# Four layers of cross attention on one core: value products of layer 0 in four column groups, operands laid out transposed ahead of the launch, and first waits moved to their first use

## What is computed

```python
h = jnp.concatenate([x, latents], axis=1)                  # x: the layer's 256 tokens, latents: see below
q = (latents @ q_w + q_b).reshape(b, k_len, NH, DH)        # 16 heads of 16
kv = (h @ kv_w + kv_b).reshape(b, p + k_len, NH, DH, 2)
kmat, v = (kv[..., 0], kv[..., 1])
attn = jnp.einsum('bkhd,bnhd->bhkn', q, kmat) / DH
attn = jnp.where(full_mask[:, None, None, :], attn, -jnp.inf)
attn = jax.nn.softmax(attn.astype(jnp.float32), axis=-1)
attn_out = jnp.einsum('bhkn,bnhd->bkhd', attn, v).reshape(b, k_len, H)
attn_out = attn_out @ out_w + out_b + residual
out = rmsnorm(attn_out, postnorm_w)
out = jax.nn.gelu(out @ mlp_w1 + mlp_b1) @ mlp_w2 + mlp_b2
return out + residual
```

## Time and profile before

| | us |
|---|---|
| median of 3 runs | 861.67 (860.86 to 862.11) |
| the profiled execution's own time | 862.19 |
| span of its profile | 860.5 |
| PE busy | 766.9 (89%) |
| DVE busy | 535.8 (62%) |
| ACT busy | 407.8 (47%) |
| POOL busy | 364.4 (42%) |

### The profile page before, as it was taken

The page is one execution under the profiler, slowest core; times in us unless marked ns, Lnnn a source line. Parts: engine busy times, 40 slices in busy tenths (PEclk is TensorE's granted clock), DMA queues, the critical chain, the costliest instruction groups (busy, mean ns, idle before and its releaser), DMA issues.

```text
span 860.5 us, 12877 instructions
## 1 busy us (share of the span) xinstructions
PE 766.9 (89%) x4759; PEld 593.1 (69%) x4759; DVE 535.8 (62%) x1035; ACT 407.8 (47%) x965; POOL 364.4 (42%) x384
## 2 busy tenths in 40 slices
PE   3899999999849978868999998999998799776798
PEld 2788887887729835546775677877577689444598
DVE  3565666657484459976553768333789647299644
ACT  1677685876522237764563322664223131266421
POOL 2565453545450148876221765000666603267300
PEclk8999999999969999999999999999999989997899
DMA  7400000000000050000254000232000000200000
GB/s 192 133 2 2 1 1 1 2 2 1 2 0 1 16 180 1 1 1 1 99 194 150 1 0 1 74 123 99 1 0 1 1 0 2 97 1 1 1 17 34
DMA packets 26050, 30.86 MB, mean 36 GB/s; under 512 B 3628, under 2 KB 20868, under 8 KB 25988
## 3 DMA queue, kind: packets, MB, share of 16 engines
q1 hardware_dynamic: 25448, 30.03, 10.8%
q10 hardware_dynamic: 540, 0.01, 0.0%
HBM read 28.98 MB, written 1.05 MB: 35 GB/s over the span
## 4 chain that ended last, share of the span: by engine, by line
PE 67%; DVE 15%; issue 7%; POOL 6%; ACT 3%; DMA 2%; ACTq 1%; SPq 0%; POOLq 0%; DVEq 0%
PE wide_ps L440 9%; PE narrow_ps L459 8%; PE narrow_ps L611 7%; PE wide_ps L758 7%; PE wide_ps L487 6%; PE narrow_ps L793 5%; PE wide_ps L709 5%; PE wide_ps L745 3%; PE wide_ps L732 3%; POOL probs L1521 2%; DVE scoresb L1231 2%; DVE mx L1240 2%; DVE sums L1247 2%; PE wide_ps L420 2%; PE wide_ps L589 2%
## 5 line engine op out<-in xcount | busy, mean ns | idle before, releaser
L916 ACT ACTIVATE probsT<-wide_ps 128x640 f32<-128x640 f32 (+1 forms) x104 | 86.0, 827 | 135.6 <-PE wide_ps L487 134.7
L1513 POOL TENSOR_TENSOR scoresb<-scoresb,mx 128x768 f32<-128x768 f32 (+1 forms) x40 | 70.7, 1767 | 151.9 <-DVE mx L1238 113.5
L1535 POOL TENSOR_TENSOR probs<-scoresb,rcp 128x512 f32<-128x512 f32 (+1 forms) x128 | 91.3, 735 | 77.9 <-DVE rcp L1315 77.9
L487 PE MATMUL wide_ps<-ident,probs 128*128 128x128 f32 x640 | 90.7, 280 | 30.0 <-POOL probs L1521 24.3
L487 PEld LDWEIGHTS wide_ps<-ident,probs 128*128 128x128 f32 x640 | 73.4, 144 | 56.7 <-issue 54.7
L1499 POOL TENSOR_TENSOR rstd<-veps,mhalf 128x1 f32<-128x1 f32 x56 | 32.0, 572 | 139.2 <-DVE veps L1166 139.2
L611 PE MATMUL narrow_ps<-probsT,vpad 128*64 128x128 f32 x640 | 83.4, 278 | 1.4 <-ACT xq L916 1.4
L1521 POOL TENSOR_TENSOR probs<-scoresb,rcp 128x1024 f32<-128x1024 f32 x40 | 78.1, 1954 | 7.3 <-DVE rcp L1248 7.3
L611 PEld LDWEIGHTS narrow_ps<-probsT,vpad 128*64 128x64 f32 x640 | 68.2, 136 | 13.7 <-issue 11.0
L440 PE MATMUL wide_ps<-xq_r,wstream_r 128*128 128x512 f32 x192 | 66.0, 427 | 8.8 <-issue 7.0
L459 PEld LDWEIGHTS narrow_ps<-wstream_r,hidden 128*128 128x128 f32 x576 | 69.2, 188 | 1.2 <-DVE xB L1194 0.5
(11 more groups left out here) (167 smaller groups left out, 1567.4 us busy)
## 6 DMA issues: line engine op xcount, KB each, us to landing
wstream<-in_L_xattn_wk SPq DMA_DIRECT2D x8, 512.0 KB, 4.1
wstream<-in_L_xattn_wv SPq DMA_DIRECT2D x8, 512.0 KB, 5.2
wstream<-in_L_xattn_wo SPq DMA_DIRECT2D x8, 512.0 KB, 6.1
wstream<-in_wqT SPq DMA_DIRECT2D x8, 512.0 KB, 7.0
wstream<-in_L_xattn_mlp_w SPq DMA_DIRECT2D x2, 1024.0 KB, 6.3
wstream<-in_L_xattn_w_fc SPq DMA_DIRECT2D x2, 1024.0 KB, 6.2
xq<-in_x SPq DMA_DIRECT2D x1, 1024.0 KB, 6.1
wstream<-in_L_xattn_fc_w SPq DMA_DIRECT2D x1, 1024.0 KB, 4.9
```

The lines of the kernel that those rows point to most:

```text
L487: m = nc.tensor.transpose(ps[:, j * P:(j + 1) * P], probs[:, u % 2, j * P:(j + 1) * P], ident[:])
L916: nc.scalar.activation(dst, src, ACT.Identity, **kw).then_inc(ring.drained[ring.slot(key)], 1)
L1513: g.tensor_tensor(s3[:, first:], s3[:, first:], mx[:, u % 3, first:].unsqueeze(2).broadcast_to([P, 16 - first, n_scores]), ALU.subtract).t ...
L1535: g.tensor_tensor(probs[:, u % 2, o:o + 2 * n].rearrange("p (i k) -> p i k", i=2), s3[:, :, lo:hi], rcp[:, u % 3, 0:2].unsqueeze(2).broadc ...
```

## The change

1. `x`, the context, the doubled context and a 128 x 384 table of all parameter columns are laid out in transposed form by `kernel()` before the launch, together with `kv_w` split into keys and values, and the ten bias rows in one array. They are loaded straight into `actT`, `ctxT`, `ctxD`, `col`, `rows`. The transposes by PE, their copies by ACT, the doubling by POOL and the zeroing of `colraw` are gone; so are the 35 loads of single vectors and nine of the ten row loads. `cols`, `ctxT` and `mask0i` are issued by ACT, the rest by SP.
2. Waits for loads stand at the first use of each tensor. 16 transposes of the identity by itself stand at the head of PE's program, one small activation at the head of ACT's.
3. The units run in the order b, half of the heads c, query half q, head pair j of four. `values0` is called every fourth step, for four units: 20 matmuls of 32 columns, the four head pairs in turn on output partitions 0, 32, 64, 96, accumulated over 5 matmuls each. The transposed probabilities stay in six buffers (`turned_probs`). `vpad0` holds 32 columns a head instead of 64.
4. Context values are made for two batches at a time (`vctx`), all at the start. The keys are spread in six pieces (`PIECES`) instead of five, the sixth in the first step of its own batch.
5. POOL adds the bias rows inside the loop (steps 4 to 19); the zeroing of `vpad0` waits for DVE's zeroing of `qhot`; `mask3` is made behind the first MLP.

```diff
-        units0 = [(b, r, q) for b in range(B) for r in range(H0 // 2) for q in range(2)]
+        units0 = [(b, 4 * c + j, q) for b in range(B) for c in range(NC) for q in range(2) for j in range(4)]
...
-        SIDE0 = [("q",), ("proj", 0), ("proj", 1), ("k", 0), ("k", 1), ("qhot", 0), ("qhot", 1), ("kpair", 0),
-                 ("kpair", 1), ("qhot", 2), ("kpair", 2), ("kpair", 3), ("qhot", 3), ("kpair", 4), ("v", 0), ("v", 1)]
...
+        SIDE0 = [("kpair", 5), ("proj", 0), ("proj", 1), ("q",), ("k", 0), ("k", 1), ("qhot", 0), ("kpair", 0),
+                 ("kpair", 1), ("qhot", 1), ("kpair", 2), ("v",), ("qhot", 2), ("kpair", 3), ("qhot", 3), ("kpair", 4)]
+        PIECES = [(0, 512), (512, 1024), (1024, 1280), (1280, 1792), (1792, 2304), (2304, 2560)]
+
+        START0 = [[("q",), ("k", 0), ("qhot", 0), ("kpair", 0), ("kpair", 1), ("qhot", 1), ("kpair", 2)],
+                  [("v",), ("vctx", 0), ("vctx", 1), ("k", 1), ("qhot", 2), ("kpair", 3), ("kpair", 4), ("qhot", 3),
+                   ("kpair", 5)]]
...
             pe.wait_ge(consts, 1)
-            pe.wait_ge(load["x"], 16)
-            turn("x0T", xA)
...
-            pe.wait_ge(load["w0"], 16 * 3)
-            pe.wait_ge(*wide.empty("ctxT"))
+            for i in range(16):
+                nc.tensor.transpose(wide_ps[:, 2, 0:P], ident[:], ident[:])
+            pe.wait_ge(load["q_w0"], 16)
...
+                elif kind == "vctx":
+
+                    ps, filled = take_narrow((job, b), 4, among)
+                    pe.wait_ge(load["ctxD"], 16)
+                    for i in range(2):
+                        for kc in range(NC):
+                            m = mm(ps[:, i * D:(i + 1) * D], ctxD[:, kc, 2 * job[1] + i, :, :].rearrange("p a k -> p (a k)"),
+                                   kv_w0[:, kc, 1, :], start=kc == 0, stop=kc == NC - 1)
...
+                for k in range(5):
+                    i, kb = k // 2, k % 2
+                    for j in range(4):
+                        r = 4 * c + j
+                        h = 2 * r + i
+                        lhs = (vpad0[b % 2][:, kb * 512 + h * 32:kb * 512 + (h + 1) * 32] if k < 4 else
+                               vctx0[b][:, r * 32:(r + 1) * 32])
+                        m = mm(ps[32 * j:32 * j + 32, qoff(q)], lhs, turned_probs(4 * group + j)[:, k * P:(k + 1) * P],
+                               start=k == 0, stop=k == 4)
...
-                if 0 <= step - 1 < n0:
-                    values0(step - 1)
+                if step > 0 and step % 4 == 0:
+                    values0(step // 4 - 1)
...
+            sp.dma_start(*halves(q_w0, t["L0_xattn_q_w"])).then_inc(load["q_w0"], 16)
+            sp.dma_start(actT[:, :, 0:S], xT[:, :, 0:S]).then_inc(load["xT0"], 16)
...
+            act.dma_start(col[:].rearrange("p a n -> p (a n)"), t["cols"]).then_inc(load["cols"], 16)
+            act.dma_start(ctxT[:], t["ctxT"].rearrange("(c p) n -> p c n", p=P)).then_inc(load["ctxT"], 16)
...
+            pool.wait_ge(qhot_zeroed, 1)
+            for lo, hi in ((0, 2048), (2048, 3072)):
+                g.memset(vpad_mem[:, lo:hi], 0.0).then_inc(vzero, 1)
...
+                if 4 <= step < 4 + NQ:
+                    add_row(step - 4, xB, xA, "L0_out_b")
+                if step == 4 + NQ:
+                    pool.wait_ge(row_added, NQ)
+                if 4 + NQ <= step < 4 + 2 * NQ:
+                    add_row(step - 4 - NQ, xA, xA, "L0_mlp_b2")
```

More of the change, by code:

```diff
@@ L60, with column_table @@
         "L3_cproj_b", "L3_proj_b"]
+def column_table():
+    at, n = {}, 0
+    for name, k in COLUMNS:
+        if n // P != (n + k - 1) // P:
+            n = -(-n // P) * P
+        at[name] = (n, k)
+        n += k
+    return at
 class Ring:
@@ L585, in scores0 @@
                     pe.wait_ge(*narrow.empty((("qhot", r // 2), b)))
-                    for piece in range(r * KEYS0 // 512, -(-(r + 1) * KEYS0 // 512)):
-                        pe.wait_ge(*narrow.empty((("kpair", piece), b)))
+                    for piece, (lo, hi) in enumerate(PIECES):
+                        if lo < (r + 1) * KEYS0 and hi > r * KEYS0:
+                            pe.wait_ge(*narrow.empty((("kpair", piece), b)))
                 for i in range(2):
@@ L633, in _ @@
                     side_product0(job, b, SIDE)
-            pe.wait_ge(load["cols"], 16 * LOADS["cols"])
-            ps, filled = take_wide("cols")
-            for i in range(2):
-                m = nc.tensor.transpose(ps[:, i * P:(i + 1) * P], colraw[:, 1 + i, :], ident[:])
-            m.then_inc(filled, 1)
+            pe.wait_ge(load["cols"], 16)
             pe.wait_ge(wk_ready, 2)
@@ L859, in _ @@
             sp.dma_start(mask3i, t["mask_BxS2_bf1"].rearrange("(a b) k -> a (b k)", a=1).broadcast_to([P, B * T])).then_inc(load["masks"], 16)
             sp.dma_start(mask1[:], t["mask_Bx1xSxS2_ff0"].rearrange("b o (h p) k -> p (b o h) k", p=P)).then_inc(load["masks"], 16)
-            for i, name in enumerate(ROWS):
-                key = name[:3] + "xattn_" + name[3:]
-                sp.dma_start(rows[:, i, :], t[key].rearrange("(a d) -> a d", a=1).broadcast_to([P, D])).then_inc(load["rows"], 16)
@@ L864, in _ @@
-            sp.wait_ge(cols_zeroed, 1)
-            for dst, src, apart in parameter_rows(False):
-                sp.dma_start(dst, src, allow_slow_non_contiguous=apart).then_inc(load["cols"], 16)
             sp.dma_start(*halves(mlp_load(0, 0), t["L0_xattn_mlp_w1"])).then_inc(load["mlp0"], 16)
@@ L959, in probs_turned @@
                 n = 5 if u < len(units0) else 8
-                evac(probsT[:, u % 2, 0:n * P], wide_ps[:, wide.slot(key), 0:n * P], wide, key)
+                evac(turned_probs(u)[:, 0:n * P], wide_ps[:, wide.slot(key), 0:n * P], wide, key)
             def side0_copy(job, b):
                 key = (job, b)
-                if job[0] in ("proj", "v"):
+                if job[0] in ("proj", "v", "vctx"):
                     return
@@ L968, in side0_copy @@
                 if job == ("qhot", 0) and b == 0:
-                    act.wait_ge(placed, 6)
+                    act.wait_ge(qhot_zeroed, 1)
                 ps = narrow_ps[:, narrow.slot(key), :]
                 if job[0] == "kpair":
-                    evac(kpair[:].rearrange("p r k -> p (r k)")[:, 512 * job[1]:512 * (job[1] + 1)], ps, narrow, key)
+                    lo, hi = PIECES[job[1]]
+                    evac(kpair[:].rearrange("p r k -> p (r k)")[:, lo:hi], ps[:, 0:hi - lo], narrow, key)
                 elif job[0] == "qhot":
@@ L1015, in keys_small @@
                     evac(kT2[:, c, :], wide_ps[:, wide.slot(key), c * 256:(c + 1) * 256], wide, key, bias=column(kb, c))
[L1017 to L1022 removed]
+            act.wait_ge(consts, 2)
+            nc.scalar.activation(rcp[:, 0, 0:1], mhalf[:], ACT.Identity)
+            act.wait_ge(load["cols"], 16)
             for job in START0[0]:
@@ L1286, in side0_copy @@
                 if job[0] == "qhot":
+                    if job == ("qhot", 0) and b == 0:
+                        dve.wait_ge(qhot_zeroed, 1)
                     v.tensor_copy(qhot[0:64, 2 * job[1]:2 * job[1] + 2, 0, :],
```

219 lines of the change are left out of this document (87 added, 132 removed).

## The result

The changed kernel takes **840.45 us** (839.04 to 842.74, 4 runs) against 861.26 (860.5 to 862.11, 4 runs): ratio 0.974, 95% interval 0.9718 to 0.9763. It is faster, as forecast, but by 21 us in place of 36, and the median is just beyond the end of the range (840). The profiled execution took 840.74 us (span 839.0) against 862.19 before: 21.45 less.

What follows compares the result with a forecast made beforehand. Waits bound the start, PE batches 0 to 2, a loop through ACT, DVE and POOL batch 3. Savings of 11.1 + 6.5 + 17.0 + 1.2 + 0.3 = 36.1 us from 862.2 gave 826.1 us, range 815 to 840.

Steps and rivals of the forecast that it cites:

- The value group: Layer 0's value products in column groups: 40 records at 0.036 us, 1.44 us in every fourth step instead of 4.96.
- the start: Stretch before the first transposes of batch 0: earlier loads and fewer waits, 11.1 us less, ends 7 to 13.5.
- POOL's row additions: Bias additions of 0.73 us each between POOL's normalizations in batch 0: priced at nothing, up to 3 us if uneven.
- batch 3 would keep its loop: Layer 0's batch 3 stays paced by the two-unit loop through ACT, DVE and POOL: 1.2 us less, 0 to 2.5.
- OVERLAP: Follow-up theory on value products: neighbours in different column groups make them cheap; without that, 3 to 4.5 us per group.
- my own case: Whole kernel: the summed savings come about as priced, 823 to 835 us; chance 55%.
- rival B: Whole kernel: in-order queues cost more, batches of 47 us, row additions 3, start 7; 19 less, 843 us; chance 15%.
- Batches 1 and 2, +4.9: Layer 0's batches 1 and 2: 43.0 us each against 51.5, together 17.0 us less, ends 21 to 9.
- all side jobs share one narrow tile: Layer 0's batches: the second key product waits while DVE empties the shared tile, 0.7 us a batch.
- the two projections: Layer 0's projection steps: POOL waits at the norm's root before the next normalization, twice; steps 1 to 4 become 2.4 us longer.
- Unchanged at about 634 us: Sign for the stretch from layer 0's last unit to the end: same length, the 7 us normalization still in it.
- 7 us faster if DVE came first: Behind layer 0, POOL's two long products hold DVE's last normalization 7.13 us; the other order would be 7 us faster.

Runs made afterwards that it cites:

- the experiment: Changed kernel with each group's 20 value products written unit by unit instead of going round the four column groups: 878.27 us.
- three remedies: Changed kernel with identity turns in batch 3, POOL's reciprocal root one step later, and layer 1's keys spread in MLP gaps: 818.04 us, ratio 0.9476.
- all places: Kernel of three remedies, first key pieces earlier, layer 3's keys in later pieces, identity turns before MLPs and layer 2's key products: 808.9 us, ratio 0.9379.

## Why the prediction was right, and where it failed

**Right.** The value group (1.44 taken, 1.23 measured, and shown by the experiment to hang on the column groups), the start (-11.1 taken, -12.4 measured; 6.3 for the first query product, 5.87 measured), and POOL's row additions at nothing. That batch 3 would keep its loop and give nearly nothing was right in kind: at full clock and with the root moved it takes 36.8 against 37.2. The sign was never close, since OVERLAP holds in chains of five.

**Half right.** 840.45 does not lie in my own case (823 to 835, 55%) but where I had put rival B (835 and above, 15%). B's own prices did not come: no batch took 47 us (44.8 and 46.1), the row additions cost nothing and the start gave 12.4 in place of 7. What came is a part of its mechanism, the waits in order, and a loss that no rival had.

**Slips that changed nothing.** Batch 3's two terms, 11 times 0.05 and 12.7 less 11.9, add to 1.35 and not to 1.2. VectorE's zeroing, put at 7.7, ended at 8.3.

**The step that failed** most stood in no term: I let TensorE's clock at 1.00 in the batches carry over to a kernel in which TensorE has pauses. "PE busy near 80% instead of 98%" was in my own list of signs (it was 83 to 85% in batches 0 to 2), without its price. What it cost, by the runs:

- *Batch 0, +1.0,* is clock: 42.04 at 0.92, and 40.9 to 41.1 at 0.96 in four runs that leave this batch as it is.
- *Batch 3, +4.7.* 2.2 vanish when TensorE is kept busy (38.45), a further 1.6 when the pause in the projection steps goes too (36.82). The last 0.8 is not settled.
- *Batches 1 and 2, +4.9.* Here a second term was too small: "all side jobs share one narrow tile", 0.7. PE's waits for DVE to empty that tile in batch 1 of the changed kernel are these three and one of 0.22:

```profile
85.85 1.13 PE L527 MATMUL narrow_ps<-actT,wstream 128*128 128x256 f32 x4 [0.43 <-DVE kparts L1252]
89.00 0.74 PE L554 MATMUL narrow_ps<-qparts,place 128*128 128x256 f32 x4 [0.79 <-DVE kparts L1252]
92.05 0.76 PE L564 MATMUL narrow_ps<-kparts,place 128*128 128x320 f32 x4 [1.47 <-DVE qhot L1260]
```

  2.69 us, and 2.26 in batch 2 (0.43, 0.43, 1.40): 3.6 more than twice 0.7. I had seen the first and not the two behind it. This is the mechanism of rival B; no run took these waits away, so that their sum is what they cost is argued and not shown. The other 1.3 is the clock in the second half of batch 2 (46.11 against 44.77 in a run where it held there). For the two projections I had 2.4; moving the root takes 2.5 off batch 1 (44.76, and 42.23 with the clock at 1.00 throughout), of which 1.6 is clock: 3.10 against 1.99 for the query product, 1.32 against 0.84 for T and scores ahead of it. So that size was right and its cause was mostly another one: the wait by itself is some 0.9, and with the root moved and a fall of the clock elsewhere in the batch it takes 43.8. As a check, batch 1 at 1.00 and with the root moved takes 42.23, where my terms without the 2.4 give 40.6: 1.6 are left that are neither clock nor root, and the waits above are the likely cause.
- *Behind layer 0, +3.4.* "Unchanged at about 634 us" failed: 839.0 - 199.3 = 639.7. The clock was 0.63 against 0.76 before, and the loss lies between the last T and POOL's start (12.85 us against 9.47); keeping the clock up in batch 3 took 3.2 us off this stretch. The collision I had left as it was did stay, at 6.35 + 7.96 in place of the earlier trace rows; my "7 us faster if DVE came first" was wrong, for DVE came first and POOL then held the next DVE instructions instead, at the same price.
- *The rest, +2.1,* is clock by the rows: the same records, PE busy 4.7 us longer. Where behind layer 0 it falls differs from run to run without an edit there: layer 1, from its query products to layer 2's first bias products, takes 95.16 us before and after, 92.41 with three remedies and 95.73 with all places.

The bound on batches (41 to 47) held the result.

## What to carry to other kernels

When work is taken off TensorE, ask what fills the time: if the clock falls in its pauses, the price is paid by whatever it does next, and turns of an identity in front of the wait can be worth several us. Of a POOL instruction of several us beside VectorE, ask where VectorE next has work; here making it smaller and later moved part of the loss, and only places where VectorE rested removed it. Doubling and removing the work in question, one run each, tells at once how close the next bound is.

## What I had not expected of the hardware

- The clock fell in the middle of a dense kernel, behind pauses in which PE was busy 1.93 and 1.44 of 4 us, and with the same instructions it fell in one run and held in another, for 1.6 us a batch.
- VectorE's cast, with one operand in SBUF, was held by POOL as long as the subtraction with two was: 6.35 and 7.96 beside products of some 7.2, 2.39 and 2.81 beside pieces that take 1.9 alone.
- With weight loads of 110 ns each and all 128 rows in use, a record takes 31 ns in changing column groups (1.23 us by 40) and 82 ns within one (3.26 by 40). The rule of the Trainium skill that the prediction weighed (TensorE: Matmul & The Clock Gate, The mechanism) has weight loads overlap running matmuls only where the row group differs. It differs in neither order here, and both take less than 110 ns a record, so the measurement decides against it.
